# The output stage of a vision kernel: where y is summed, when its loads are issued, and which tokens share a partition

## The reference: what is computed

```python
ys = ys + Ds.reshape(1, K_DIRS, d, 1) * xs
y = _cross_merge(ys, h, w)          # row-order scans + column-order scans, transposed back
y = jnp.transpose(y, (0, 2, 1))     # channels last
mu = jnp.mean(y, -1, keepdims=True)
var = jnp.mean(jnp.square(y - mu), -1, keepdims=True)
y = (y - mu) * jax.lax.rsqrt(var + LN_EPS) * ln_weight + ln_bias
```

## Time and profile before

| what | value |
|---|---|
| time, median of 3 runs | 21461.23 us (21459.94 to 21463.92) |
| time of the profiled execution | 21461.03 us |
| its span in the trace | 21459.2 us |
| output stage in the trace | from 20543 us to the end, 916 us |
| period of one image in it | 55.37 us |
| DMA share of the stage | 68.9% of 16 engines, 154.39 MB |
| granted clock of TensorE in the stage | 0.50 to 0.53 |

### The profile page before, as it was taken

One profiled execution on the slowest core, in us unless ns is written; L12 is line 12 of the kernel. 1 busy time (PEld: TensorE's weight loads), 2 busy tenths in 40 slices (PEclk: granted clock), 3 DMA queues, 4 the chain that ended last, 5 costly groups with the idle time before them and its releaser, 6 DMA issues. The chain is left out here.

```text
span 21459.2 us, 289980 instructions
## 1 busy us (share of the span) xinstructions
PE 16247.2 (76%) x83096; PEld 5502.1 (26%) x83096; DVE 19058.9 (89%) x21113; ACT 10090.7 (47%) x19239; POOL 15280.9 (71%) x5892
## 2 busy tenths in 40 slices
PE   8999999999977777777777777777777777777731
PEld 5555555522211111111111111111111111111111
DVE  5555555589989999999999999999999999999966
ACT  4444444467754444444444444444444444444410
POOL 0000000056669999999999999999999999999977
PEclk9999999989987777777777777777777777777755
DMA  1000000056666666666666666666666666666666
GB/s 22 18 18 18 18 18 18 18 195 226 229 196 129 127 134 131 128 132 130 129 134 131 127 132 132 129 131 131 128 133 133 127 130 133 130 131 133 127 147 166
DMA packets 1129481, 2520.46 MB, mean 117 GB/s; under 512 B 247606, under 2 KB 448824, under 8 KB 1112960
## 3 DMA queue, kind: packets, MB, share of 16 engines
q1 hardware_dynamic: 1128320, 2508.11, 52.3%
HBM read 2000.43 MB, written 507.38 MB: 117 GB/s over the span
## 5 line engine op out<-in xcount | busy, mean ns | idle before, releaser
L1235 POOL TENSOR_TENSOR c_pr<-c_hs,c_c_u 128x1568 f32<-128x1568 f32 x3072 | 9934.9, 3238 | 1037.5 <-DVE c_hs L1199 762.2
L1133 ACT ACTIVATE c_psum<-c_dt_u,c_a_neg 128x784 f32<-128x784 f32 x6144 | 5641.7, 918 | 7475.1 <-DVE c_hs L1199 7422.3
L1199 DVE TENSOR_TENSOR_SCAN c_hs<-c_psum,c_dbx 128x785 f32<-128x785 f32 (+1 forms) x4352 | 7616.3, 1773 | 20.2 <-issue 20.2
L1065 PE MATMUL c_psum<-c_pr,c_red 128*64 128x392 f32 x24576 | 7211.0, 705 | 1.0 <-POOL c_pr L1235 1.0
L1054 PE MATMUL c_psum<-c_br_u,c_sel 48*128 48x512 bf16 (+1 forms) x8704 | 2965.6, 433 | 4029.9 <-DVE c_dbx L1176 3927.8
L1176 DVE TENSOR_TENSOR c_dbx<-c_u_u,c_psum 128x784 f32<-128x784 f32 x4352 | 4103.1, 943 | 40.0 <-PE c_psum L1054 40.0
L1224 POOL TENSOR_TENSOR c_dbp<-c_u_u,c_bp_u 128x784 f32<-128x784 f32 x1792 | 3316.1, 1850 | 105.2 <-DVE c_hs L1199 62.6
L1199 DVE TENSOR_TENSOR_SCAN c_hs<-c_psum,c_dbp 128x785 f32<-128x785 f32 (+1 forms) x1792 | 3191.5, 1781 | 0.0
L196 POOL TENSOR_TENSOR a_xpb<-a_x_sb,a_pb_sb 98x768 f32<-98x768 f32 x128 | 231.2, 1807 | 4063.4 <-DVE a_x L285 4049.3
L1065 PEld LDWEIGHTS c_psum<-c_pr,c_red 128*64 128x64 f32 x24576 | 1789.8, 177 | 3404.6 <-issue 3132.1
L1054 PEld LDWEIGHTS c_psum<-c_br_u,c_sel 48*128 48x128 bf16 x8704 | 522.0, 101 | 8204.3 <-DVE c_dbx L1176 7011.4
(11 more groups left out here) (119 smaller groups left out, 17351.5 us busy)
## 6 DMA issues: line engine op xcount, KB each, us to landing
c_c_u<-scr_bc SPq DMA_DIRECT2D x512, 1568.0 KB, 28.9
c_dt_u<-scr_dt SPq DMA_DIRECT2D x512, 588.0 KB, 7.4
c_u_u<-scr_u SPq DMA_DIRECT2D x512, 588.0 KB, 11.2
c_bp_u<-scr_bc SPq DMA_DIRECT2D x512, 588.0 KB, 22.0
scr_dt<-p_dt_o SPq DMA_DIRECT2D x384, 392.0 KB, 3.0
scr_u<-p_u_o SPq DMA_DIRECT2D x384, 392.0 KB, 2.4
scr_y<-c_y_sb SPq DMA_DIRECT2D x256, 294.0 KB, 17.8
d_yin<-scr_y SPq DMA_DIRECT2D x32, 2352.0 KB, 15.5
```

What stands on the lines that cost most here:

```text
L1065: mm = pe.matmul(Y(3 * w + q)[64 * h:64 * h + 64, :], red[:], pr[:, s % RP, HT * h:HT * h + HT], start=(p == 0 and opens(w)), stop=(p == N ...
L1133: nc.scalar.activation(dA(s)[:, data], dt_u[:, d, s // NPR, :], ACT.Exp, scale=a_neg[:, k, s:s + 1]).then_inc(exp_done, 1)
L1199: nc.vector.tensor_tensor_scan(hs[:, s % RH, way], dA(s)[:, way], added, 0.0, ALU.mult, ALU.add).then_inc(scan_done, 1)
L1235: nc.gpsimd.tensor_tensor(pr[:, s % RP:s % RP + 2, :], hs[:, s % RH:s % RH + 2, data], c_u[:, d, s % NPR:s % NPR + 2, :], ALU.mult).then_i ...
```

## The change

The work on y is shared out anew. VectorE comes first and adds dsum * x to the row-order sum in place (`with_x`, line 1383 of the changed kernel), and GpSimd adds the column-order sum and writes `yf` (`total`, line 1350). `yf` has two buffers, `par` = 0 or 1 by image. Both passes for image b + 1 are written inside image b, the first half at group 2 and the second at group 5 (`SUMS`). SP issues the loads of image b + 2 inside image b, each behind the y sum that frees its buffers, with the stores of image b between them. Multiplying by w moves from GpSimd to VectorE, which writes (y - mean) * w (`centre`, line 1406). Multiplying by rstd moves to ScalarE, four passes of 112 x 192 a group (`scale`). GpSimd keeps the sum with b (`shift`, line 1357). A tile takes every fourth token of the group's 448, so that partition p holds tokens 4p to 4p + 3 and a store moves one piece of 3072 bytes per partition, where it moved four of 768 bytes. TensorE then reads `yf` with a step of four floats.

```diff
-        yf = sb("yf", [HC, 2, L])
+        yf = sb("yf", [HC, 2, 2, L])
...
+        SUMS = (2, 5)
...
+            def body(b, par, left):
                 for g in range(NGRP):
-                    sp.wait_ge(o_done, NGRP * b + g + 1)
-                    dst = out[bass.ds(b, 1), TT * GT * g:TT * GT * (g + 1), :].rearrange("u (t p) c -> p (u t) c", p=TT)
-                    sp.dma_start(dst, ob[:, g].rearrange("p (t c) -> p t c", t=GT)).then_inc(o_out[g], 16)
+                    if left > 1 and g in SUMS:
+                        a = SUMS.index(g)
+                        sp.wait_ge(yf_done, 2 * b + a + 3)
+                        load(b + 2, a)
+                    if g >= 1:
+                        store(b, g - 1)
+                    elif not (isinstance(b, int) and b == 0):
+                        store(b - 1, NGRP - 1)
+                if not left:
+                    store(b, NGRP - 1)
+
+            def store(b, g):
+                sp.wait_ge(o_done, NGRP * b + g + 1)
+                dst = out[bass.ds(b, 1), TT * GT * g:TT * GT * (g + 1), :].rearrange("u (p t) c -> p (u t c)", p=TT)
+                sp.dma_start(dst, ob[:, g]).then_inc(o_out[g], 16)
...
-                for a in range(2):
-                    pool.wait_ge(y_in[a], 48 * b + 48)
-                    rows = yin[:, a, 0].rearrange("p (h w) -> p h w", h=IMG)
-                    nc.gpsimd.tensor_tensor(rows, rows, yin[:, a, 1].rearrange("p (w h) -> p h w", h=IMG),
-                                            ALU.add).then_inc(add_done, 1)
+            def total(b, par, a):
+                if a == 0 and not (isinstance(b, int) and b < 2):
+                    pool.wait_ge(t_full, NGRP * b - NGRP)
+                pool.wait_ge(dx_done, 2 * b + a + 1)
+                rows = lambda t: t.rearrange("p (h w) -> p h w", h=IMG)
+                nc.gpsimd.tensor_tensor(rows(yf[:, par, a]), rows(yin[:, a, 0]), yin[:, a, 1].rearrange("p (w h) -> p h w", h=IMG),
+                                        ALU.add).then_inc(yf_done, 1)
+
+            def shift(b, g):
+                n = NGRP * b + g
+                pool.wait_ge(sc_done, n + 1)
+                o = ob[:, g].rearrange("p (t c) -> p t c", t=GT)
+                nc.gpsimd.tensor_tensor(o, o, b_sb[:].unsqueeze(1).to_broadcast([TT, GT, C]), ALU.add).then_inc(o_done, 1)
+
+            def body(b, par, left):
                 for g in range(NGRP):
...
+                    if g >= 1:
+                        shift(b, g - 1)
+                    elif not (isinstance(b, int) and b == 0):
+                        shift(b - 1, NGRP - 1)
+                    if left and g in SUMS:
+                        total(b + 1, 1 - par, SUMS.index(g))
+                if not left:
+                    shift(b, NGRP - 1)
...
-                    nc.vector.scalar_tensor_tensor(yf[:, a], x_in[:, a], dsum[:, a:a + 1], yin[:, a, 0],
-                                                   ALU.mult, ALU.add).then_inc(yf_done, 1)
+            def with_x(b, a):
+                dve.wait_ge(y_in[a], 48 * b + 48)
+                nc.vector.scalar_tensor_tensor(yin[:, a, 0], x_in[:, a], dsum[:, a:a + 1], yin[:, a, 0],
+                                               ALU.mult, ALU.add).then_inc(dx_done, 1)
...
+                def centre(g):
                     dve.wait_ge(o_out[g], 16 * b + 16)
+                    dve.wait_ge(ag_done, NGRP * b + g + 1)
                     for t in range(GT):
-                        ins = nc.vector.tensor_scalar(ob[:, g, C * t:C * t + C], tile_ps(g, t), mv[:, g, t, 0:1],
-                                                      rstd[:, g, t:t + 1], ALU.subtract, ALU.mult)
+                        ins = nc.vector.scalar_tensor_tensor(ob[:, g, C * t:C * t + C], tile_ps(g, t), mv[:, g, t, 0:1],
+                                                             w_sb[:], ALU.subtract, ALU.mult)
                     ins.then_inc(nm_done, 1)
 
                 for g in range(NGRP):
                     stat(g)
                     if g:
-                        normalise(g - 1)
-                normalise(NGRP - 1)
-
-            images(dve, body)
+                        centre(g - 1)
+                    if left and g in SUMS:
+                        with_x(b + 1, SUMS.index(g))
+                centre(NGRP - 1)
...
+            def scale(b, g):
+                n = NGRP * b + g
+                act.wait_ge(rs_done, n + 1)
+                act.wait_ge(nm_done, n + 1)
+                for t in range(GT):
+                    o = ob[:, g, C * t:C * t + C]
+                    ins = nc.scalar.activation(o, o, ACT.Copy, scale=rstd[:, g, t:t + 1])
+                ins.then_inc(sc_done, 1)
...
                         for a in range(2):
-                            tok = TT * (GT * g + t)
-                            mm = pe.transpose(tile_ps(g, t)[:, HC * a:HC * a + HC], yf[:, a, tok:tok + TT], id_sb[:])
+                            tok = slice(TT * GT * g + t, TT * GT * (g + 1), GT)
+                            mm = pe.transpose(tile_ps(g, t)[:, HC * a:HC * a + HC], yf[:, par, a, tok], id_sb[:])
                     mm.then_inc(t_full, 1)
```

More of the change, by code:

```diff
@@ L1282, in build_output, with halves @@
         block = ctx.enter_context(nc.Block())
+        SUMS = (2, 5)
+        def halves(eng, body):
+            body(0, 0, min(n_img - 1, 2))
+            if n_img > 4:
+                with eng.Fori(0, n_img // 2 - 2) as i:
+                    body(2 * i + 1, 1, 2)
+                    body(2 * i + 2, 0, 2)
+            if n_img > 2:
+                body(n_img - 3, 1, 2)
+                body(n_img - 2, 0, 1)
+            body(n_img - 1, 1, 0)
         @block.sync
@@ L1305, in _ @@
             if n_img > 1:
-                with sp.Fori(0, n_img - 1) as b:
-                    for a in range(2):
-                        sp.wait_ge(yf_done, 2 * b + a + 1)
-                        load(b + 1, a)
-                    stores(b)
-            stores(n_img - 1)
+                for a in range(2):
+                    sp.wait_ge(yf_done, a + 1)
+                    load(1, a)
+            halves(sp, body)
             for g in range(NGRP):
                 sp.wait_ge(o_out[g], 16 * n_img + 16)
-        def images(eng, body):
-            body(0, True)
-            if n_img > 1:
-                with eng.Fori(1, n_img) as b:
-                    body(b, False)
         @block.gpsimd
@@ L1349, in _, with body @@
             dve.wait_ge(ready, 2)
-            def body(b, first):
-                for a in range(2):
-                    n = 2 * b + a
-                    dve.wait_ge(add_done, n + 1)
-                    if a == 0 and not first:
-                        dve.wait_ge(t_full, NGRP * b)
-                    nc.vector.scalar_tensor_tensor(yf[:, a], x_in[:, a], dsum[:, a:a + 1], yin[:, a, 0],
-                                                   ALU.mult, ALU.add).then_inc(yf_done, 1)
+            def with_x(b, a):
+                dve.wait_ge(y_in[a], 48 * b + 48)
+                nc.vector.scalar_tensor_tensor(yin[:, a, 0], x_in[:, a], dsum[:, a:a + 1], yin[:, a, 0],
+                                               ALU.mult, ALU.add).then_inc(dx_done, 1)
+            def body(b, par, left):
+                first = isinstance(b, int) and b == 0
                 def stat(g):
@@ L1384, in body @@
                     if g:
-                        normalise(g - 1)
-                normalise(NGRP - 1)
-            images(dve, body)
+                        centre(g - 1)
+                    if left and g in SUMS:
+                        with_x(b + 1, SUMS.index(g))
+                centre(NGRP - 1)
+            with_x(0, 0)
+            with_x(0, 1)
+            halves(dve, body)
         @block.scalar
```

51 lines of the change are left out of this document (24 added, 27 removed).

## The result

| what | before | after |
|---|---|---|
| time, median of 4 runs each, in turns on one chip | 21461.42 us (21459.94 to 21463.92) | 21221.82 us (21220.53 to 21222.1) |
| ratio after / before | | 0.9888, 95% interval 0.9871 to 0.9905 |
| span in the trace | 21459.2 us | 21218.7 us |
| period of an image | 55.37 us | 39.8 us |
| DMA share of the stage | 68.9% | 90.2% |

The change saves 239.6 us, or 1.1%.

The account below looks back on a forecast made before the run. A serial chain per image bounded the old stage; GpSimd plus VectorE's two-input passes would bound the new. Start 20593.1, 15 periods of 41.0 (615.0) and tail 31.1 give span 21239.2, forecast 21241 us, range 21222 to 21282.

Parts of the forecast that it names:

- rival A: The forecast: GpSimd and the shared passes set the period, 40.1 to 42.2 us; 21228 to 21259 us; chance 0.62.
- T: Moment when an image's second y sum ends; the steps follow the cycle to the next such moment, T + 41.0.
- Step 1: Group 0 of an image is centred at T + 6.8: 6.5 us as before plus 0.3 for TensorE's step.
- Steps 4 to 7: Both `with_x` passes at 3.4 us, GpSimd's sums with b and y sums between them, from T + 10.2 to T + 41.0.
- The tail: Last image after T, without y work for a next image: to last centred group, ScalarE, GpSimd and store, 31.1 us.
- D: More overlap than allowed, down to the DMA queue's 38.8 us a period: 21208 to 21228 us; chance 0.12.
- step 3: GpSimd adds b to group 0, 1.8 us, done at T + 10.2, after 4.8 us with nothing to do.
- E: Slower than before through TensorE's loads with a step; at 1.1 us per transpose 61.6 a period, about 21560; chance 0.03.
- step 6: `with_x` for the second half, 3.4 us, gets in as the first half's y sum ends; done at T + 27.2.
- step 4: `with_x` for the first half, 3.4 us, after waiting for GpSimd; done at T + 13.6.
- B: The DMA queue becomes the bound, a period of 42.4 to 44.5 us: 21262 to 21294 us; chance 0.14.
- C: `centre` also waits for GpSimd, a period of 49 to 52 us: 21361 to 21409 us; chance 0.06.

Follow-up runs that it names:

- a2: Changed kernel with TensorE reading 112 neighbouring tokens of yf without a step, stores left as they are: 21222.31 us.
- a8: Changed kernel plus one unread VectorE pass per image but the last, with two inputs in SBUF, behind the last `centre`: 21243.68 us.
- a5: Changed kernel with the y sums at groups 0 and 4, and x loaded for image 0 alone: 21153.81 us.
- a4_sums_04: Changed kernel with the next image's y sums at groups 0 and 4 instead of 2 and 5: 21174.94 us, ratio 0.9866.
- a6: Changed kernel, y sums still at groups 2 and 5, with x loaded for image 0 alone: 21223.1 us.
- b2: Kernel before with the product with w on VectorE and that with rstd on ScalarE; old order and single `yf`: 21363.99 us.
- a3: Changed kernel with the product with w back on GpSimd and rstd on VectorE; order, two buffers and early loads kept: 21358.62 us.
- a1: Changed kernel with the old token order, stores of 768-byte pieces and TensorE reading without a step: 21223.22 us, ratio 0.9889.
- b1: Kernel before with only the new layout: four neighbouring tokens per partition, 3072-byte stores, TensorE step of four: 21462.33 against 21461.14 us.
- c1: Changed kernel with y sums at groups 0 and 4 and the old layout, stores in 768-byte pieces: 21180.94 us.
- a7: Changed kernel with the long part of x loaded a second time into a buffer nobody reads: 21322.6 us.
- a4_sums_14: Changed kernel with the next image's y sums at groups 1 and 4 instead of 2 and 5: 21180.21 us, ratio 0.9867.
- c2: Changed kernel with y sums at groups 0 and 4, and SP's store ahead of the load at those groups: 21199.14 us.

## Why the prediction was right in kind and missed its range

The forecast of rival A was the mechanism, and it held point by point. The table puts the timeline of the changed kernel beside the steps, with T = 21022.25 + 8.35 = 21030.60.

| step | forecast | measured | difference of the step's own length |
|---|---|---|---|
| 1, group 0 centred | T + 6.8 | T + 6.25 | -0.55 |
| 2, ScalarE | T + 8.4 | T + 7.92 | +0.07 |
| 3, b to group 0 | T + 10.2 | T + 9.73 | 0.01 |
| 4, first D * x | T + 13.6 | T + 13.01 | -0.12 |
| 5, b to group 1 | T + 15.4 | T + 14.66 | -0.15 |
| 5, y sum | T + 23.8 | T + 23.00 | -0.06 |
| 6, second D * x | T + 27.2 | T + 26.28 | -0.12 |
| 7, b to groups 2 to 4 | T + 32.7 | T + 31.46 | -0.32 |
| 7, y sum | T + 41.0 | T + 39.78 | 0.02 |

**What failed.** The steps are right in kind, and the terms were sized too large, in three places.

- Step 1: "I add 0.3 for TensorE's new step of four floats." It costs nothing (`a2`), since group 0 is transposed at a granted clock of 0.50, where a load takes 213 ns with the step and 217 without. The other 0.23 us is `centre`, taken at the 1.60 us of line 1378, where four of them take 1.37. The Trainium skill, page "SBUF — State Buffer", section "Door 1: The DMA port swizzle (why `[64,N]` ≈ `[32,N]`)", has each access that crosses to a new line of 16 bytes pay, and the same note gives four fp32 as how far one can stride for free, so the page leaves this step open. The traces decide: 208 against 134 ns at 1.00, nothing at 0.50. The reason that I gave for staying near the lower end, half the clock, pointed the right way, and the term should have been zero. The doubling in the earlier trace rows, at 0.90, fits with that; it was for the moving operand and a step of 56 floats, and whether these two matter as well wasn't tried.
- Steps 4 to 7: hand-overs. I took 3.4 us for a D * x pass in turn and 0.1 us between GpSimd's passes. But the earlier trace rows already had 11.46 - 8.18 = 3.28, and 3.28 is what it takes, since the start of the waiting instruction lies beside the end of the other. GpSimd's pass behind it gains likewise: 1.65 instead of 1.8. With the y sums counted in these are 0.75 us a period.
- The tail: 31.1 forecast, 21218.7 - 21189.58 = 29.1 measured. The last group was centred at T + 21.8 instead of T + 24.0: 0.55 of that is step 1, 1.2 that two `centre` are 2.88 apart and not 3.12, and the rest that the last one follows at once; ScalarE's last pass ended 2.2 behind it and not 1.6, and the store was 0.4 shorter.

The sum: 15 periods of 39.81 instead of 41.0 are -17.8 us, the start (20592.4 for 20593.1) -0.7, the tail -2.0, together -20.5 of the span, which is the forecast's 21239.2 less the 21218.7 measured. In the time it is 19 us, since the traced execution is 1.3 us below the median.

**The range.** A's lower bound of 40.1 us a period let three costs shrink (ScalarE, the step, one hand-over), but held `centre` at 1.60 and the other hand-overs fixed. Its place is 39.8. The range then cut D at a third, at 21222, and the time was 21221.82. The result lies where D was, and for D's reason only in part: D needed GpSimd's idle time at step 3 to shrink, and it is 4.36 us where I wrote 4.8, which is 0.44 of the 1.2 us. What the range left out was also more than the "about 0.2" that I wrote: by the chances, spread evenly over their ranges, it is 0.26. And E's 61.6 us a period would make 21550 us, not 21560; neither slip moves the forecast.

**Who comes next.** "So a waiting VectorE pass gets in between two GpSimd instructions" came from one place of the second stage. It held at step 6 in all 15 images, and so the cycle came out; at step 4 GpSimd had no pass ready. It is no rule: in `a8` the y sum went ahead of the waiting pass in all 15 images, and in `a5` sums with b did. What decides between them stays open.

**The DMA queue.** "An image costs 2 x 15.9 + 7 x 1.0 = 38.8 us" was too high for a queue that has stores and loads in it. It needs 37.0 when full (`a4_sums_04`) and was busy for 37.8 in the changed kernel. It stayed hidden, as forecast, with 2 us to spare (`a6`), so this error did not touch the time. It did touch two of the later expectations.

**The rivals.** B fell by `a6`. C fell by the 380 to 419 ns of `centre`. E fell by `a2`, and by the 5.38 us of 32 transposes, where the earlier trace rows had 5.36; even at the upper clock level the step adds 74 ns to a load, far from the 0.56 us by which E needed a transpose to grow. D is above.

**What each part gave.** The split alone saves 97.9 us (`b2`), the order with its buffers and early loads alone 102.5 (`a3`), the order of the tokens nothing (`a1`, `b1`), and the two that count together 39 more than their sum.

**What the change leaves on the table.** With `SUMS = (0, 4)` the kernel takes 21174.94 us, 47 less than the changed kernel, with four runs each that don't overlap, on two chips, and a period of 36.8 in place of 39.8 us. The floor behind it is 21153.81, where the queue is relieved (`a5`).

**What stays open.** Why the full queue moves 265, 260, 259, 254 and 247 GB/s in `c1`, `a4_sums_04`, `a7`, `a4_sums_14` and `c2`, where loads alone made 227 and stores alone 346. The price that fits best is by bytes at about 260, not by loads and stores apart; `c2`, where the stores go first, is the exception. And why the periods at (0, 4) vary from 34.4 to 39.8 us from image to image, while those of (2, 5) and of `a5` are even: only the share of 1.01 goes with it.

## What to carry to other kernels

When two engines share work, first find which instructions exclude each other, then add their times as if they were one engine: here GpSimd's passes and VectorE's two-input passes make 35.4 us an image, and that sum, not either busy share, was the floor. An edit that shortens a chain and one that lightens the engine behind it are each worth less alone than together. Where a second resource is close behind, moving the gap by one number (`SUMS`) gained 47 us until the DMA queue was full, and which transfer then waits in it decides who stands still.

## What the runs showed of the hardware

- An instruction that stands still for the other engine is recorded as running: 12.68 us for a pass of 3.29 (`a8`), 4.98 for one of 1.80 (`a3`). Busy time of GpSimd and VectorE is thus no measure of work: GpSimd's is 400.00 of 400 us in `a5`, of which some 6 of each 35.4 are standing.
- A VectorE pass that waits gets in between two GpSimd instructions in some places and not in others. In the changed kernel it did, behind the first y sum of each image: the longest D * x pass is 4.74 us, less than 3.28 and one pass of 1.8. In `a8` an 8.34 us y sum went ahead of it (12.68 us for a pass of 3.29), in `a5` sums with b did (7.06 us). The pass costs GpSimd 3.2 us in `a3` and `a8`, although the D * x pass is recorded at 3.48 alone.
- A weight load of 112 columns with a step of four floats took 213 ns, without it 217, at a granted clock of 0.50, the lower of the two levels (1.2 GHz). At 1.00, the upper level (2.4 GHz), it took 208 with the step and 134 without, and eight of them together 0.93 us and 0.68.
- Stores in pieces of 768 and of 3072 bytes made no difference that can be measured, with a queue that has slack (21462.33 and 21461.14 us) or none (21180.94 and 21174.94).
